# Second layer of the 128-slot expert jobs as three float32r passes over split weights and split inputs, with thirteen weight places

## The reference, cut to what matters

```
x = x + _L0_ffn_ref(_layernorm(x), Wr, br, W1, b1, W2, b2)

logits = xt @ Wr + br                       # 512 tokens, 8 experts
top_vals, top_idx = top_k(logits, 2)
gate = softmax over the two chosen logits
h = relu(xt @ W1[e] + b1[e])                # 512 -> 2048
y = h @ W2[e] + b2[e]                       # 2048 -> 512
out = sum over the two chosen experts of gate * y
```

## Time and profile before

| what | us |
|---|---|
| median of 3 runs | 1077.27 (1074.42 to 1077.58) |
| the profiled execution | 1076.48 |
| its span in the trace | 1074.7 |
| job 0 begins (first hidden matmul) | 798.56 |
| job 3, the first narrow one, begins | 920.9 |
| jobs 3 to 7 on TensorE | 920.9 to 1064.4 |

### The profile page before, as it was taken

How to read it: one execution, slowest core, us unless ns; L and a number is a source line. 1 busy time by engine, 2 the same in 40 slices (tenths; PEclk the granted TensorE clock), 3 DMA queues, 4 the chain that set the end, 5 groups by cost and what they waited for, 6 DMA issues and landing times.

```text
span 1074.7 us, 17658 instructions
## 1 busy us (share of the span) xinstructions
PE 1003.0 (93%) x7131; PEld 786.4 (73%) x7138; DVE 552.5 (51%) x1149; ACT 434.5 (40%) x565; POOL 260.3 (24%) x223
## 2 busy tenths in 40 slices
PE   7899999999999998999999999767869999999996
PEld 6488777888777886777888777443459999977773
DVE  4234985465885556885454983588951111211110
ACT  3111786161785164786151785368611101111110
POOL 0301840001830001740001830698210101100000
PEclk9899999999999999999999999889959999999998
DMA  7182871523962514771431953600069978899800
GB/s 274 39 148 77 191 176 46 198 79 88 197 154 66 234 49 137 177 181 46 149 103 35 199 116 131 262 1 1 34 213 386 375 275 286 285 339 312 242 11 13
DMA packets 76923, 169.91 MB, mean 158 GB/s; under 512 B 6440, under 2 KB 16808, under 8 KB 71968
## 3 DMA queue, kind: packets, MB, share of 16 engines
q1 hardware_dynamic: 74720, 163.87, 50.0%
q0 software_dynamic: 2112, 4.80, 2.0%
HBM read 119.01 MB, written 16.10 MB: 126 GB/s over the span
## 4 chain that ended last, share of the span: by engine, by line
PE 78%; DVE 7%; DMA 4%; issue 4%; POOL 3%; ACT 2%; SPq 1%; DVEq 0%; POOLq 0%; ACTq 0%
PE psum L2082 11%; PE psum L455 9%; PE psum L435 7%; PE psum L2112 6%; PE psum L470 5%; PE psum L2097 5%; PE psum L391 5%; PE psum L374 5%; PE psum L393 5%; PE psum L392 5%; PE psum L375 5%; PE psum L376 5%; DMA ctx_raw<-in_ctx_t 2%; PE psum L423 1%; DMA lower<-in_lower 1%
## 5 line engine op out<-in xcount | busy, mean ns | idle before, releaser
L876 POOL CAST stack<-kT 128x2048 fp32r<-128x2048 f32 x32 | 63.1, 1980 | 409.1 <-ACT kT L752 397.5
L622 DVE CUSTOM_DVE_ANT_0 prob<-psum,biasmap,top 128x512 f32<-128x512 f32 x192 | 144.2, 751 | 22.8 <-PE psum L435 13.6
L790 ACT ACTIVATE prob<-prob,top 128x2048 f32<-128x2048 f32 x64 | 128.6, 2009 | 33.4 <-DVE top L622 33.1
L455 PE MATMUL psum<-ident,prob 128*128 128x128 f32 x1024 | 134.8, 274 | 7.1 <-ACT probT L798 4.3
L455 PEld LDWEIGHTS psum<-ident,prob 128*128 128x128 f32 x1024 | 116.3, 141 | 28.1 <-issue 12.4
L2082 PE MATMUL psum<-xT,wring 128*128 128x128 f32 (+3 forms) x1024 | 134.0, 292 | 0.6 <-ACT xT L2364 0.6
L2082 PEld LDWEIGHTS psum<-xT,wring 128*128 128x128 f32 x1024 | 131.9, 193 | 2.8 <-issue 1.9
L752 ACT COPY kT<-psum 128x512 f32<-128x512 f32 x64 | 37.6, 587 | 198.3 <-PE psum L376 191.7
L798 ACT COPY probT<-psum 128x1024 f32<-128x1024 f32 x96 | 96.6, 1011 | 51.9 <-PE psum L470 50.0
L2271 DVE TENSOR_SCALAR hidden<-psum,b 128x128 f32<-128x128 f32 (+3 forms) x64 | 23.6, 369 | 161.2 <-PE psum L2082 161.2
L391 PE MATMUL psum<-wv_hi,ctx_part 128*128 128x512 f32 x256 | 100.4, 392 | 0.0
(11 more groups left out here) (248 smaller groups left out, 1550.4 us busy)
## 6 DMA issues: line engine op xcount, KB each, us to landing
wring<-in_w SPq DMA_DIRECT2D x64, 1024.0 KB, 9.3
ctx_raw<-in_ctx_t SPq DMA_DIRECT2D x15, 1024.0 KB, 6.1
stack<-stack SPq DMA_DIRECT2D x32, 256.0 KB, 4.7
early_stack<-early_stack SPq DMA_DIRECT2D x28, 256.0 KB, 5.0
ternary<-ternary_weights SPq DMA_DIRECT2D x1, 6272.0 KB, 24.3
prob<-in_w_gate_t SPq DMA_DIRECT2D x1, 5632.0 KB, 17.5
stack<-key_stack SPq DMA_DIRECT2D x20, 256.0 KB, 4.0
query_stacks<-prob SPq DMA_DIRECT2D x16, 256.0 KB, 5.4
```

The lines of the kernel that those rows point to most:

```text
L455: mm = pe.transpose(psum[:, w + i, j * P:(j + 1) * P], prob[:, prob_slot(n, j), kt * P:(kt + 1) * P], ident[:, :])
L622: dve.tensor_tensor_reduce(prob[:, slot, keys], psum[:, scores.of[n, j, c], :], biasmap[:, keys], 1.0, top[:, h, (c + 1) % 2:(c + 1) % 2 + ...
L790: act.activation(prob[:, slot, :], prob[:, slot, :], ACT.Exp, bias=top[:, h, 1:2], scale=-1.0, accum_out=top[:, h, 2:3]).then_inc(*raised. ...
```

## The change

- The weight ring has 13 places instead of 16. The place of piece i of job q is (8 q + i) mod 13, and a piece waits for the use of the piece 13 before it.
- The second layer of narrow jobs reads W2 as a high part, in four places of its own (`w_high`, one for each W2 piece of a job), and a low part, which is written over the raw piece in its ring place (`w_low` lies on `wring`). The activations are split into `h_high` and `h_low` (`h_low` lies on `hidden`). 16 matmuls of float32 become 48 of float32r.
- ScalarE writes the high parts, VectorE the low parts: W2 in halves of 128x1024, hidden in groups of four tiles, 128x512. The first four halves of a job are split while the job before is in its second layer; the later four, and the hidden groups, stand between the evictions of the job's own hidden tiles.
- `add_b2(0)` and `add_b2(1)` come ahead of the bias product on VectorE.

```diff
-        wring = sb("wring", [P, 2 * PIECES, DT, D], F32)
+        PLACES, HIGHS = 13, DT
+        region_raw = ExitStack()
+        wring = [sb(f"wring{i}", [P, DT, D], F32, region_raw) for i in range(PLACES)]
+        region_raw.close()
+        w_low = [sb(f"w_low{i}", [P, DT, D], F32R) for i in range(PLACES)]
+        w_high = [sb(f"w_high{i}", [P, DT, D], F32R) for i in range(HIGHS)]
...
+        HALVES_OF = [(j, s) for j in range(DT) for s in range(2)]
...
+        LATER_HALVES = {4: (2, 0), 6: (2, 1), 8: (3, 0), 10: (3, 1)}
...
+        def place_of(q, i):
+            return (PIECES * q + i) % PLACES
...
                 for h in range(HT):
-                    piece = PIECES * (q % 2) + DT + h // 4
-                    pe.wait_ge(*hidden_ready(q, h))
-                    if h % 4 == 0:
-                        pe.wait_ge(*weights_in[piece].at(q, DT + h // 4))
-                    mm = pe.matmul(psum[0:width, w, :], hidden[:, h, 0:width], wring[:, piece, h % 4, :],
-                                   start=(h == 0), stop=(h == HT - 1))
+                    j, row = h // 4, h % 4
+                    if row == 0:
+                        pe.wait_ge(*h_low_made.at(q, j))
+                    if row % 2 == 0:
+                        pe.wait_ge(*low_made.at(q, j, row // 2))
+                    high, low = w_high[j][:, row, :], w_low[place_of(q, DT + j)][:, row, :]
+                    pe.matmul(psum[0:width, w, :], h_high[:, h, 0:width], high, start=(h == 0), stop=False)
+                    pe.matmul(psum[0:width, w, :], h_high[:, h, 0:width], low, start=False, stop=False)
+                    mm = pe.matmul(psum[0:width, w, :], h_low[:, h, 0:width], high, start=False, stop=(h == HT - 1))
...
+            def low_weights(q, j, s):
+                dve.wait_ge(*high_made.at(q, j, s))
+                at = place_of(q, DT + j)
+                dve.tensor_tensor(w_low[at][:, rows_of(s), :], wring[at][:, rows_of(s), :],
+                                  w_high[j][:, rows_of(s), :].bitcast(F32),
+                                  ALU.subtract).then_inc(*low_made.made(q, j, s))
+
+            def low_hidden(q, g):
+                width = JOBS[q][2]
+                dve.wait_ge(*h_high_made.at(q, g))
+                dve.tensor_tensor(h_low[:, 4 * g:4 * g + 4, 0:width], hidden[:, 4 * g:4 * g + 4, 0:width],
+                                  h_high[:, 4 * g:4 * g + 4, 0:width].bitcast(F32),
+                                  ALU.subtract).then_inc(*h_low_made.made(q, g))
...
                         hidden_tile(q, h)
+                        if not wide(q):
+                            if h in LATER_HALVES:
+                                low_weights(q, *LATER_HALVES[h])
+                            if h >= 4 and h % 4 == 0:
+                                low_hidden(q, h // 4 - 1)
+                    if not wide(q):
+                        low_hidden(q, DT - 1)
                     if q + 1 < end:
                         copy_rows(q + 1)
                         gate_slots(q + 1)
-                    for k in range(0, DT if wide(q) else 0, 2):
-                        copy_yT(q, k)
+                    ahead = list(HALVES_OF[:4]) if q + 1 < end and not wide(q + 1) else []
+                    for k in range(0, DT, 2):
+                        for half in ahead[k:k + 2]:
+                            low_weights(q + 1, *half)
+                        if wide(q):
+                            copy_yT(q, k)
...
+            add_b2(0)
+            add_b2(1)
             dve.tensor_tensor(b1_at[:, :, :, :],
...
-            add_b2(0)
-            add_b2(1)
...
+            def high_weights(q, j, s):
+                at = place_of(q, DT + j)
+                if s == 0:
+                    act.wait_ge(*arrived(q, DT + j))
+                    if q - 1 in narrows:
+                        act.wait_ge(*(w2_used.at(q - 1, j) if j < DT - 1 else y_done.at(q - 1, 0)))
+                act.copy(w_high[j][:, rows_of(s), :], wring[at][:, rows_of(s), :]).then_inc(*high_made.made(q, j, s))
+
+            def high_hidden(q, g):
+                width = JOBS[q][2]
+                act.wait_ge(*hidden_v.at(q, 4 * g + 2))
+                act.wait_ge(*hidden_a.at(q, 4 * g + 3))
+                act.copy(h_high[:, 4 * g:4 * g + 4, 0:width],
+                         hidden[:, 4 * g:4 * g + 4, 0:width]).then_inc(*h_high_made.made(q, g))
...
                         hidden_tile(q, h)
+                        if not wide(q):
+                            if h % 4 == 3:
+                                high_hidden(q, h // 4)
+                            if h + 1 in LATER_HALVES:
+                                high_weights(q, *LATER_HALVES[h + 1])
                     if q + 1 < end:
                         copy_rows(q + 1)
-                    for k in range(1, DT if wide(q) else 0, 2):
-                        copy_yT(q, k)
+                    ahead = list(HALVES_OF[:4]) if q + 1 < end and not wide(q + 1) else []
+                    for k in range(1, DT, 2):
+                        for half in ahead[k - 1:k + 1]:
+                            high_weights(q + 1, *half)
+                        if wide(q):
+                            copy_yT(q, k)
                     if not wide(q):
                         gate_output(q)
...
-                if q >= 2:
-                    if i < DT:
-                        sp.wait_ge(*hidden_done.at(q - 2, 4 * i + 3))
+                if PIECES * q + i >= PLACES:
+                    used, part = divmod(PIECES * q + i - PLACES, PIECES)
+                    if part < DT:
+                        sp.wait_ge(*hidden_done.at(used, 4 * part + 3))
```

More of the change, by code:

```diff
@@ L1984, in wide @@
             return JOBS[q][2] > P
-        routed_v = events("routed_v", ["apart", "chosen", "meta", "order", "gate", "load", "b1",
-                                       *(("out", b) for b in tokens)])
+        routed_v = events("routed_v", ["apart", "chosen", "meta", "order", "gate", "load", ("out", 0), ("out", 1), "b1",
+                                       ("out", 2), ("out", 3)])
         routed_t = events("routed_t", ["places", "gatesT", *(("b2", b) for b in tokens)])
@@ L1996, in perceiver_block @@
         wides = [q for q in each if wide(q)]
-        weights_in = [events(f"piece{i}_in", [(q, i % PIECES) for q in each if q % 2 == i // PIECES], 16)
-                      for i in range(2 * PIECES)]
+        pieces = [(q, i) for q in each for i in range(PIECES)]
+        weights_in = [events(f"piece{i}_in", pieces[i::PLACES], 16) for i in range(PLACES)]
+        narrows = [q for q in each if not wide(q)]
+        HALVES_OF = [(j, s) for j in range(DT) for s in range(2)]
+        high_made, low_made = (events(name, [(q, *half) for q in narrows for half in HALVES_OF])
+                               for name in ("high_made", "low_made"))
+        h_high_made, h_low_made = (events(name, [(q, g) for q in narrows for g in range(DT)])
+                                   for name in ("h_high_made", "h_low_made"))
         picks = events("picks", each)
@@ L2070, in hidden_tile @@
             def hidden_tile(q, h):
-                width, piece = JOBS[q][2], PIECES * (q % 2) + h // 4
+                width, piece = JOBS[q][2], place_of(q, h // 4)
                 w, free = hidden_banks.take(("hidden", q, h), hidden_ready(q, h))
@@ L2077, in hidden_tile @@
                 if h % 4 == 0:
-                    pe.wait_ge(*weights_in[piece].at(q, h // 4))
+                    pe.wait_ge(*arrived(q, h // 4))
                 if free:
@@ L2081, in hidden_tile @@
                 for k in range(DT):
-                    mm = pe.matmul(psum[:, w, 0:width], wring[:, piece, k, h % 4 * P:(h % 4 + 1) * P],
+                    mm = pe.matmul(psum[:, w, 0:width], wring[piece][:, k, h % 4 * P:(h % 4 + 1) * P],
                                    xT[:, q % 2, k, 0:width], start=(k == 0), stop=(k == DT - 1))
@@ L2091, in output_wide @@
                     for h in range(HT):
-                        piece = PIECES * (q % 2) + DT + h // 4
+                        piece = place_of(q, DT + h // 4)
                         if k == 0:
@@ L2095, in output_wide @@
                             if h % 4 == 0:
-                                pe.wait_ge(*weights_in[piece].at(q, DT + h // 4))
-                        mm = pe.matmul(y_place(q, k), wring[:, piece, h % 4, k * P:(k + 1) * P], hidden[:, h, 0:width],
+                                pe.wait_ge(*arrived(q, DT + h // 4))
+                        mm = pe.matmul(y_place(q, k), wring[piece][:, h % 4, k * P:(k + 1) * P], hidden[:, h, 0:width],
                                        start=(h == 0), stop=(h == HT - 1))
@@ L2301, in jobs @@
                         mark_picks(q + 1)
+                    if q == first and not wide(q):
+                        for half in HALVES_OF[:4]:
+                            low_weights(q, *half)
                     for h in range(0, HT, 2):
@@ L2395, in jobs @@
```

(20 more changed lines are left out.)

17 lines of the change are left out of this document (13 added, 4 removed).

## The result

The changed kernel takes 1068.35 us in the median of 7 runs (1063.15 to 1070.85), the kernel before 1077.27, also of 7 runs: a ratio of 0.9915, 95% interval 0.9891 to 0.9939. Measured again beside the last experiment it is 0.9896 (0.9873 to 0.9918). The forecast was 1066.6 in 1061 to 1072. The profiled execution took 1068.35 for a span of 1066.5.

A forecast was written before the change was run, and what follows sets the result against it. TensorE, busy 1003 of 1074.7 us, was taken as the bound. From the profiled 1076.48 us, -14.3 (matmuls) + 2.6 (place of splits) + 3.3 (row gather) - 1.5 (start) = -9.9 gave 1066.6, range 1061 to 1072.

The forecast's parts named there:

- The matmuls: Second layer of five narrow jobs: 48 float32r matmuls at 0.2267 us, 10.88 instead of 13.74 us a job, -14.3 us.
- Splitting, its price: Narrow jobs: subtractions 1.22 and 0.69 us, copies 1.04 and 0.618; 12.5 us more on VectorE, 10.8 on ScalarE, covered on average.
- Splitting, its place: Hidden stage of narrow jobs: late evictions hold PSUM banks for tiles 9 and 13, 0.55 us a job, 0.4 in job 7, +2.6.
- The row gather: Narrow jobs 3 to 6: later row ids, then gather and VectorE subtractions delay each other; +3.3 us, bounds 0 and 8.
- The start: Start of job 0: b2 additions first, so the first gather takes 1.1 instead of 2.76 us; -1.5, bounds 0 and -1.7.
- The bias term: Start of job 0: after two b2 additions, VectorE steps of 1.22 and 1.22 us give b1 at 796.0, before rows are turned.
- Jobs 0 to 2: Wide jobs: no term of their own in the sum; first-layer code unchanged and 13 ring places needed still less, cost 0.
- The ring: Weight ring with 13 places instead of 16: cost 0, upper bound about 3 us from late weights in four jobs.
- (a): Rival: POOL and VectorE don't meet, the first gather was long because it was first; no 3.3, no -1.5; 1064.8 us, chance 0.25.
- (b): Rival: a late W2 piece or late rows stop evictions and gating, taking half the gain; 1069.5 to 1072 us, chance 0.17.
- (c): Rival: slower, the bank ring bounds as VectorE subtractions take 1.86 instead of 1.22 us beside POOL; 1081 us, chance 0.04.
- (d): Rival: all splitting hidden, the schedule slack by a few tenths; -14.3 - 1.5, 1060.7 us, chance 0.04.

The follow-up runs named there:

- the last experiment: The version with early ids measured again, in the same rounds as the changed kernel: 1064.74 us, ratio 0.9868 to the kernel before.
- early ids: Against the changed kernel, VectorE in narrow jobs writes the next job's row ids right after hidden tile 4, ahead of the first split half: 1062.72 us, ratio 0.9865.
- the second pair: Changed kernel and early ids, both measured again without edit in the same rounds: 1067.47 us (ratio 0.9896) and 1064.74 us (0.9868).
- the first two experiments: Each against the changed kernel: early ids, 1062.72 us; the two b2 additions put back behind the bias product and sum, 1069.11 us in one run.

## Why the prediction was right

By its own steps, in its order:

**The matmuls** (-14.3). Job 5's second layer lasts 11.10 us (992.51 to 1003.61), a pace of 0.231, not 0.2267. That is -2.64 a job and **-13.2** in five, so this term was 1.1 too large. The form was priced by the right rows, and this kernel's operands run 2% slower.

**Splitting, its price** (1.22, 1.04, 0.69, 0.62). Measured 1.221, 1.044, 0.686 and 0.619 in the groups above. Right.

**Splitting, its place** (+2.6). This was too high: what is left beside the matmuls and the rows is about +0.4. VectorE in job 4:

```profile
956.33 1.22 DVE L2308 TENSOR_TENSOR w_low<-wring,w_high 128x1024 fp32r<-128x1024 f32 x1 [0.81 <-ACT w_high L2439]
957.47 0.68 DVE L2315 TENSOR_TENSOR h_low<-hidden,h_high 128x512 fp32r<-128x512 f32 x1
958.07 0.22 DVE L2271 TENSOR_SCALAR row_id<-psum 128x1 uint32<-128x1 f32 x1
958.21 0.34 DVE L2302 TENSOR_SCALAR hidden<-psum,b 128x128 f32<-128x128 f32 x1
958.46 1.22 DVE L2308 TENSOR_TENSOR w_low<-wring,w_high 128x1024 fp32r<-128x1024 f32 x1
959.60 0.34 DVE L2302 TENSOR_SCALAR hidden<-psum,b 128x128 f32<-128x128 f32 x1
960.18 1.22 DVE L2308 TENSOR_TENSOR w_low<-wring,w_high 128x1024 fp32r<-128x1024 f32 x1 [0.24 <-ACT w_high L2439]
...
961.92 0.35 DVE L2302 TENSOR_SCALAR hidden<-psum,b 128x128 f32<-128x128 f32 x1
```

The order is the one that was forecast, tile 4 to tile 10. But each operation starts about 0.1 before the recorded end of the one before (958.21 + 0.34 ends at 958.55, the next starts at 958.46), so the nine operations from low (2,0) to tile 10, laid end to end, come out 0.5 late or more. Tile 10 ended at 962.27, 11.6 into the job, not 12.15. TensorE was stopped for 0.1 at tile 13, and not at tile 9. The step that failed is the sum of durations end to end. With early ids the first layer and rows take 14.86, against 14.91 before the change, and nothing is left of the 0.55.

**The row gather** (+3.3). The sum was near, and the mechanism half right. POOL in the changed kernel:

```profile
792.55 1.34 POOL L2510 DMA_INDIRECT xg<-xm_rows,row_id  x1 [12.20 <-DVE row_id L2271]
794.20 0.97 POOL L2510 DMA_INDIRECT xg<-xm_rows,row_id  x1 [0.30 <-issue]
959.21 1.43 POOL L2510 DMA_INDIRECT xg<-xm_rows,row_id  x1 [5.30 <-DVE row_id L2271]
986.02 1.44 POOL L2510 DMA_INDIRECT xg<-xm_rows,row_id  x1 [5.08 <-DVE row_id L2271]
```

Ids ended at 7.6 and the gather started at 8.54; the forecast had 7.8 and 8.7. It took 1.43 instead of 1.09 as (2,1) ran beside it, and rows were there at 15.05, forecast 14.4 to 15.1. What failed is the other half. Low (3,0) at 960.18 took 1.22 although POOL worked until 960.64, so the gather did not delay the bank. In job 3 the second scatter was not delayed either: it had begun before low (2,0) and took its 1.35. TensorE therefore came earlier than forecast, at 14.6, and waited for rows (the idle time stands in brackets):

```profile
955.08 10.19 PE L2110 MATMUL psum<-xT,wring 128*128 128x128 f32 x88
965.72 0.66 PE L2094 MATMUL psum<-ident,xg 128*128 128x128 f32 x4 [0.45 <-DMA xg<-xm_rows,row_id]
```

Such waits were 0.36, 0.45, 0 and 0.60 us in jobs 3 to 6; after one the transposes take 0.2 us more. Early ids price the whole at 2.4 us (133.35 less 130.94) and, in the second pair, at 3.3 (134.28 less 130.95). The hold itself is the smaller part: 1.43 instead of 1.09 in three jobs that waited, about 1 us by estimate, and the rest is that the ids came late.

The Trainium skill (SBUF — State Buffer, "SBUF: two separate sides") has the exclusive lock between the two engines, and the places where a gather began within a subtraction or product agree with it: 2.76, 1.94, 1.43 against 0.97 to 1.35 alone. The half by which VectorE is blocked when it comes second shows at none of the gathers and scatters. The prediction read the page so that the gather goes free, because a subtraction of two SBUF tiles blocks only a GpSimd operation that reads SBUF. The measurement decides against that reading. The rows name `row_id`, a tile in SBUF, among the gather's inputs, so the page's rule may cover it; that this read is what was held is not shown.

**The start** (-1.5). It came to -0.7. The gather did drop from 2.76 to 1.34, and the second one began 1.4 earlier after the first weight load. But it landed 3.69 after its start, not 3.0, which takes back 0.7: in the 3 us from 793.5 on the DMA still moved 395 GB/s of weights and rows, where in the kernel before it moved 154 in the 3 us from 793.2 on. The bias term was wrong too: the product takes 1.85 by itself, not 1.22, so b1 was ready at 798.98, as late as the rows: by itself it would have held the start near where it is. VectorE, then the chain:

```profile
794.66 1.29 DVE L2334 TENSOR_TENSOR x<-psum,x 128x512 f32<-128x512 f32 x2 [2.30 <-PE psum L2188]
795.87 1.85 DVE L2393 TENSOR_TENSOR b_at<-b_all,same 128x1024 f32<-128x1024 f32 x1
797.76 1.22 DVE L2399 TENSOR_REDUCE b<-b_at 128x128 f32<-128x1024 f32 x1
```

```profile
794.20 3.69 DMA xg<-xm_rows,row_id
797.93 1.13 PE psum L2094 x4
800.30 9.41 PE psum L2110 x40
```

**Jobs 0 to 2** (0). They came to +0.5. Job 0 took 0.8 more, all of it in its first five tiles: 40 records took 9.41 us against 8.66 in the chain of before. The granted clock rose from 1.2 to 2.4 GHz 5.5 us after the first matmul, before the change 3.9 us after it, and 1.6 us more at half the clock are 0.8. In the other runs of the new kernels it rose 4.6 to 5.4 us after, so a part of this is chance. Job 1 took 0.3 less, as with 13 places alone.

**The ring** (0). Right for jobs 3 to 7, by its own run; in job 1 it gave the 0.3.

**Sum.** The expert part was forecast at -9.9 and is -10.7: matmuls -13.2, rows +2.4, rest of the narrow jobs +0.4, start -0.7, jobs 0 to 2 +0.5. Chance ahead of it gave the profiled execution 2.4 back, and the medians moved by 8.9. That the sum came so near is in part luck: its terms were off by +1.1 (matmuls), -2.2 (place of the splits), -0.9 (rows), +0.8 (start) and +0.5 (jobs 0 to 2), and these nearly cancel. Of the rivals, (a) fell with the first two experiments, (b) did not come: late rows cost 2.4 us, inside the forecast's own term, and no weights were late as long as TensorE had three passes. (c) fell with the 1.221 of 40 subtractions, and (d), all hidden, is nearly what early ids make of the kernel.

## What to carry to other kernels

When work is put into the gaps of an engine that also writes the indices of a gather, write them first: the gather's lead time was worth 2.4 to 3.3 us, the 12 us of VectorE work added to each job next to nothing. Don't let a VectorE operation on two SBUF tiles begin just before POOL issues an indirect DMA: here the gather waited for the rest of it. After a TensorE saving look for the next bound before saving more: here the weight stream at 379 GB/s holds a job at 22.2 us, by one run.

## What was not expected of the hardware

- The lock costs in one direction only: a gather that began within a VectorE operation on two SBUF tiles ended 0.95 to 1.2 us after that operation, while the VectorE operations beside POOL's gathers and scatters kept 1.21 to 1.23, whichever began first. A scatter that began 0.23 before the subtraction kept its 1.35.
- A VectorE product of 128x1024 with its innermost run of 8 elements broadcast took 1.85 us, a plain subtraction of that size 1.22, with nothing on POOL in either case. What makes the difference was not tried.
- The same float32r matmul runs every 227 ns in attention and every 228 to 236 ns here, by operand address and order of passes.
- The kernel's times scatter by 4 to 8 us from run to run, and the traces put 5.5 us of it ahead of the experts.
